# GpSimd subtracts the least of each late round, ScalarE takes four heads' exponentials at once, and the passage and the second norm are ordered anew

## The reference

```python
# 1. neighbourhood attention, 8 heads of 16, window 7 x 7, gate, residual, norm with gain and bias
attn = einsum(q, kn) + rpb_bias;  a = softmax(attn over the 49 keys)
y = x + (einsum(a, vn) @ proj_w + proj_b) * sigmoid(relu(x @ g1_w + g1_b) @ g2_w + g2_b)
t = norm(y) * ln_g + ln_b
# 2. additive attention over the 1024 tokens of an image, on n = norm(t)
h = tanh(q[:, :, None, :] + k[:, None, :, :] + bh)      # 32 units for each pair of tokens
e = einsum('biju,u->bij', h, Wa) + ba
t = t + softmax(e) @ n
# 3. top-1 mixture of 8 experts (128 -> 512 -> 128, relu) with a capacity, on norm(t)
t = t + ffn(norm(t))
```

## Time and profile before

| | us |
|---|---|
| median of 3 runs (714.23 to 714.83) | 714.52 |
| the profiled execution | 713.9 |
| its span | 712.1 |

### The profile page before, as it was taken

The page is one execution under the profiler, slowest core; times in us unless marked ns, Lnnn a source line. Parts: engine busy times, 40 slices in busy tenths (PEclk is TensorE's granted clock), DMA queues, the critical chain, the costliest instruction groups (busy, mean ns, idle before and its releaser), DMA issues.

```text
span 712.1 us, 12354 instructions
## 1 busy us (share of the span) xinstructions
PE 548.5 (77%) x4512; PEld 272.0 (38%) x4512; DVE 516.3 (73%) x1442; ACT 571.3 (80%) x364; POOL 506.1 (71%) x588
## 2 busy tenths in 40 slices
PE   6997835999898969798939577676776666758994
PEld 3665621434343434354304122221231222237783
DVE  2677767877989797888865896977878778633456
ACT  3675637899999997999977999999999999920531
POOL 1002167997979778998998998989798798611474
PEclk9999975999999989899988899999999999977998
DMA  8600100100000000000800000000000000001400
GB/s 307 211 2 2 60 1 1 60 1 5 1 12 3 12 0 14 1 9 5 323 0 13 0 12 9 5 12 1 13 9 4 12 10 5 10 3 34 132 25 27
DMA packets 14108, 24.32 MB, mean 34 GB/s; under 512 B 1296, under 2 KB 11058, under 8 KB 13024
## 3 DMA queue, kind: packets, MB, share of 16 engines
q1 hardware_dynamic: 12640, 20.63, 8.5%
q0 software_dynamic: 1408, 2.91, 1.2%
HBM read 16.79 MB, written 7.37 MB: 34 GB/s over the span
## 4 chain that ended last, share of the span: by engine, by line
PE 32%; issue 21%; DVE 21%; ACT 17%; POOL 8%; DMA 1%; DVEq 0%; POOLq 0%; SPq 0%; ACTq 0%
ACT front L1148 15%; PE ps L895 9%; POOL front L581 5%; DVE front L1427 5%; PE ps L693 3%; PE ps L1056 3%; PE ps L1046 3%; PE ps L915 2%; DVE back L1236 2%; PE ps L722 2%; PE ps L741 2%; PE ps L732 1%; DVE back L1263 1%; POOL y_all L540 1%; PE ps L938 1%
## 5 line engine op out<-in xcount | busy, mean ns | idle before, releaser
L1148 ACT ACTIVATE front<-front 128x4096 f32<-128x4096 f32 x128 | 454.9, 3605 | 36.8 <-POOL front L581 24.9
L581 POOL TENSOR_SCALAR front<-k,q 128x1024 f32<-128x1024 f32 (+1 forms) x464 | 413.5, 908 | 42.3 <-PE ps L895 33.5
L895 PE MATMUL ps<-front,cst 128*32 128x512 f32 x2048 | 261.0, 630 | 80.4 <-ACT front L1148 73.5
L1427 DVE TENSOR_SCALAR front<-ps,q 128x512 f32<-128x512 f32 (+1 forms) x256 | 213.8, 878 | 22.0 <-PE ps L895 17.4
L895 PEld LDWEIGHTS ps<-front,cst 128*32 128x32 f32 x2048 | 55.9, 113 | 200.3 <-ACT front L1148 99.8
L1088 ACT ACTIVATE back<-back,mn 128x320 f32<-128x320 f32 (+1 forms) x128 | 62.4, 537 | 14.2 <-DVE mn L1236 14.2
L540 POOL TENSOR_SCALAR y_all<-y_all,mvs,lny 128x128 f32<-128x128 f32 x15 | 11.7, 786 | 74.2 <-DVEq L1392 58.9
L1236 DVE CUSTOM_DVE_ANT_0 back<-ps,back 128x320 f32<-128x320 f32 (+1 forms) x128 | 54.0, 469 | 12.5 <-PE ps L693 10.4
L1459 DVE COPY ptm<-ps 128x512 f32<-128x512 f32 x32 | 22.1, 692 | 38.2 <-PE ps L906 36.7
L693 PE MATMUL ps<-conv 32*128 32x320 f32 (+1 forms) x256 | 38.3, 477 | 4.9 <-DVE mn L1236 4.8
L1263 DVE COPY back<-ps 128x512 f32<-128x512 f32 x44 | 30.2, 686 | 7.5 <-PE ps L732 7.3
(11 more groups left out here) (146 smaller groups left out, 658.9 us busy)
## 6 DMA issues: line engine op xcount, KB each, us to landing
back<-in_w SPq DMA_DIRECT2D x2, 2048.0 KB, 10.8
xbuf<-rec SPq DMA_DIRECT2D x1, 2720.0 KB, 21.3
back<-in_top SPq DMA_DIRECT2D x2, 1024.0 KB, 6.2
back<-in_bottom SPq DMA_DIRECT2D x2, 1024.0 KB, 6.5
front<-xbuf SPq DMA_DIRECT2D x2, 720.0 KB, 7.0
back<-in_inner SPq DMA_DIRECT2D x1, 1280.0 KB, 10.6
back<-in_b SPq DMA_DIRECT2D x1, 1280.0 KB, 16.1
xT<-in_xT SPq DMA_DIRECT2D x4, 256.0 KB, 6.4
```

The lines of the kernel that those rows point to most:

```text
L581: last = nc.gpsimd.tensor_scalar(ring[u % DEPTH][:, at + lo:at + hi], k4[:, img * L + k0 + lo:img * L + k0 + hi], q4[:, m:m + 1], 1.0, ALU ...
L895: last = nc.tensor.matmul(bank(to)[c * U:(c + 1) * U, :], c_("wa", U - QPG - QPG * row, 2 * U - QPG - QPG * row), ring[t % DEPTH][:, at:at ...
L1148: nc.scalar.activation(ring[t % DEPTH], ring[t % DEPTH], ACT.Tanh).then_inc(h_ready, 1)
L1427: last = nc.vector.tensor_scalar(ring[u % DEPTH][:, at + lo:at + keys], ps[:, base + k0 + lo:base + k0 + keys], q4[:, m:m + 1], None, ALU.add)
```

## The change

- Passage: units 0 and 4 (`BIASED`) have no sums; ScalarE takes their tanh from the keys with the query as bias, in eight operations of 512. The transposes of the first four rows and their copy move from round 15 to round 14. The first keys are copied by VectorE from another bank. VectorE's part ahead of the loop is a list of its own, and the steps before 0 are gone; the loops begin at step 0, and on GpSimd and VectorE at step 1.
- Second norm: rows 4 and 5 are GpSimd's, 6 and 7 VectorE's; 8 to 11 as before but a row per step on GpSimd; 12 and 13, then 14, on GpSimd; 15 on VectorE. Tokens and keys of the last pack are turned four steps earlier, and image 1's units may have sums from `project_step(15)` + 5 on instead of + 9.
- Late rounds: GpSimd computes (least - score) for each head (`below_most`), two heads in step begin+1 and two in begin+2, after the step's sums; ScalarE then has one exponential over the four heads, in step begin+3.

```diff
+BIASED = (0, CH // 2)
 def sums_at(t):
-    gate = lambda u: FIRST if u < NEW_KEYS[1] else KEYS_1 if u < NEW_KEYS[2] else project_step(NB - 1) + 9
-    return [u for u in range(T) if max(u - DEPTH + 1, gate(u)) == t]
+    gate = lambda u: KEYS_1 if u < NEW_KEYS[2] else project_step(NB - 1) + 5
+    return [u for u in range(NEW_KEYS[1] + 1, T) if max(u - DEPTH + 1, gate(u)) == t]
...
-        middle, late_rows = project_step(11), project_step(NB - 1)
+        rows_8, rows_12, rows_14, rows_15 = (project_step(j) + 1 for j in (11, 13, 14, 15))
...
# GpSimd
-            scale_rows(2, 4, 7)
-            weigh_rows("lng", ALU.mult, 4, 7)
-            weigh_rows("lnb", ALU.add, 4, 7, done=True)
+            scale_rows(2, 4, 6)
+            weigh_rows("lng", ALU.mult, 4, 6)
+            weigh_rows("lnb", ALU.add, 4, 6, done=True)
...
+            def below_most(rho, pair):
+                n = KEYS[kind_of(rho // 2)]
+                pool.wait_ge(n_ready, NG * rho + 2 * pair + 2)
+                for g in range(2 * pair, 2 * pair + 2):
+                    p = prob[rho % 3][:, g, 0:n]
+                    last = nc.gpsimd.tensor_scalar(p, p, mn[rho % 3][:, g:g + 1], -1.0, ALU.subtract, ALU.mult)
+                last.then_inc(below_ready, 1)
...
-            for t in range(FIRST, END):
+            key_query_sums(1)
+            key_query_sums(2)
+            normal_rows(2, 4, 6)
+            key_query_sums(3)
+            for t in range(KEYS_1, END):
...
+                for pair in range(2):
+                    rho = round_at(t - 1 - pair, begin)
+                    if rho is not None:
+                        below_most(rho, pair)
-                if t == middle + 4:
-                    scale_rows(3, 8, 12)
+                if rows_8 + 2 <= t < rows_8 + 6:
+                    scale_rows(3, t - rows_8 + 6, t - rows_8 + 7)
...
# TensorE, after the early rounds
+            pe.wait_ge(n_ready, NG * RS)
+            query_columns(0, 1)
             values(RS - 1)
-            query_columns(0, 1)
+            key_half(0, 2)
+            sums(BS - 1)
+            query_key_rows("wqe", 2, 3, q_done)
+            spread(BS - 1)
+            pe.wait_ge(pta_ready, chunks_before(RS) - RS)
+            query_key_rows("wqo", 2, 4, q_done)
+            project(BS - 1)
             pe.wait_ge(ptd_ready, RS)
-            pe.wait_ge(pta_ready, chunks_before(RS) - RS)
-            key_half(0, 5)
-            query_key_rows("wqe", 2, 2, q_done)
-            query_key_rows("wqo", 2, 3, q_done)
-            query_key_rows("wk", 2, 4, k_done)
+            query_key_rows("wk", 2, 5, k_done)
...
# ScalarE
+                if t in BIASED:
+                    ...
+                    for at, k0, keys, m, _, _ in tiles_of_unit(t):
+                        last = nc.scalar.activation(ring[t % DEPTH][:, at:at + keys], k4[:, k0:k0 + keys], ACT.Tanh,
+                                                    bias=q4[:, m:m + 1])
+                    last.then_inc(h_ready, 1)
+                    return
...
+            def soften_late(rho):
+                p = prob[rho % 3][:, :, 0:KEYS[kind_of(rho // 2)]]
+                act.wait_ge(below_ready, 2 * (rho - RS) + 2)
+                nc.scalar.activation(p, p, ACT.Exp).then_inc(p_ready, NG)
...
-                rho = round_at(t - 2, begin)
-                if rho is not None:
-                    soften(rho, (0, 1))
                 rho = round_at(t - 3, begin)
                 if rho is not None:
-                    soften(rho, (2, 3))
+                    soften_late(rho)
...
# VectorE, ahead of its loop
+            keys_out(0, 2)
+            inverse(BS - 1)
+            dve.wait_ge(ln_rows, 2)
+            dve.wait_ge(y_ready, 7)
+            row_stats(4, 7)
+            scaled(BS - 1)
+            key_query_sums(1)
+            gated(BS - 1)
+            dve.wait_ge(y_ready, BS)
+            row_stats(7, 8)
+            scale_late(0, 4, 8)
+            dve.sem_inc(ln_last, 1)
+            link.end()
+            normal_rows(y_all, 6, 8)
+            key_query_sums(2)
+            weigh_rows(6, 8)
+            row_stats(6, 8)
+            key_query_sums(3)
+            scale_late(0, 6, 8)
+            link.end()
+            normal_rows(x_all, 6, 8)
+            dve.sem_inc(t_ready[1], 1)
```

More of the change, by code:

```diff
@@ L189, in sums_at, with summed @@
 def sums_at(t):
-    gate = lambda u: FIRST if u < NEW_KEYS[1] else KEYS_1 if u < NEW_KEYS[2] else project_step(NB - 1) + 9
-    return [u for u in range(T) if max(u - DEPTH + 1, gate(u)) == t]
+    gate = lambda u: KEYS_1 if u < NEW_KEYS[2] else project_step(NB - 1) + 5
+    return [u for u in range(NEW_KEYS[1] + 1, T) if max(u - DEPTH + 1, gate(u)) == t]
+def summed(u):
+    return u + 1 - sum(k <= u for k in BIASED)
 def leasts_before(n):
@@ L447, in keys_whole, with keys_bank @@
             return GROUPS[GROUP_AT[u]].half is None
-        KEYS_NEEDED = [1, 2, 4]
+        KEYS_NEEDED = {BIASED[0] + 1: 1, BIASED[1] + 1: 2, T // 2: 4}
+        def keys_bank(u):
+            g = GROUPS[GROUP_AT[u]]
+            return 2 * 512 if g.block >= BPI or g.half == 0 else 4 * 512
         def pool_part(u, n):
@@ L610, in _ @@
                     normed(p)
[L611 to L613 removed]
+                for pair in range(2):
[4 more added lines that the diff above has]
+                    scale_rows(3, t - rows_8 + 6, t - rows_8 + 7)
+                if t == rows_8 + 6:
                     weigh_rows("lng", ALU.mult, 8, 12)
[L615 removed]
+                if t == rows_8 + 7:
                     weigh_rows("lnb", ALU.add, 8, 12, done=True)
[L617 to L625, removed]
+                if rows_8 + 10 <= t < rows_8 + 14:
+                    normal_rows(3, t - rows_8 - 2, t - rows_8 - 1)
+                if rows_12 + 1 <= t < rows_12 + 3:
+                    scale_rows(4, t - rows_12 + 11, t - rows_12 + 12)
+                if t == rows_12 + 3:
+                    weigh_rows("lng", ALU.mult, 12, 14)
+                    weigh_rows("lnb", ALU.add, 12, 14, done=True)
+                if rows_12 + 5 <= t < rows_12 + 7:
+                    normal_rows(4, t - rows_12 + 7, t - rows_12 + 8)
+                if t == rows_14 + 1:
+                    scale_rows(5, 14, 15)
+                    weigh_rows("lng", ALU.mult, 14, 15)
+                    weigh_rows("lnb", ALU.add, 14, 15, done=True)
+                if t == rows_14 + 3:
+                    normal_rows(5, 14, 15)
             def weighted_bias(q):
@@ L820, in turn_tokens @@
             def turn_tokens(half, to):
-                pe.wait_ge(t_ready[half], 2 if half == 1 else 1)
+                pe.wait_ge(t_ready[half], (1, 2, 4, 4)[half])
                 for k in range(4):
@@ L938, in keep_clock @@
                     nc.tensor.matmul(bank(3, 0, P), c_("ident"), c_("tri"), start=True, stop=True)
-            for t in range(FIRST, END):
+            for t in range(END):
                 rho = round_at(t, begin)
@@ L1156, in soften_main @@
                 nc.scalar.activation(pm[:, lo:L], pm[:, lo:L], ACT.Exp, bias=nmin[:, :], scale=-1.0).then_inc(pm_ready, 1)
-            for t in range(FIRST, END):
-                if 0 <= t < T:
+            for t in range(END):
+                if t < T:
                     hidden_units(t)
+                if t == 0:
+                    query_rows(1, 0, 0, 3)
+                    query_rows(1, 0, 1, 4)
+                    act.wait_ge(k_done, 3)
+                    nc.scalar.activation(kT[:, 0:512], bank(5), ACT.Identity, bias=c_("bk")).then_inc(k_ready, 1)
                 p = query_block(t, 2)
@@ L1533, in _ @@
                 if t == KEYS_1:
-                    tokens_out(1, 2)
+                    tokens_out(1, 3)
                     dve.wait_ge(q4_done, 2)
-                    nc.vector.tensor_scalar(q4[:, P:2 * P], bank(3, 0, P), c_("bh"), None, ALU.add).then_inc(q4_ready, 1)
+                    nc.vector.tensor_scalar(q4[:, P:2 * P], bank(2, 0, P), c_("bh"), None, ALU.add).then_inc(q4_ready, 1)
                     keys_out(1, 5)
```

166 lines of the change are left out of this document (74 added, 92 removed).

## The result

The changed kernel takes 780.12 us (median of 4 runs, 775.75 to 781.94) against 714.67 of the kernel before: 1.090 times (95% interval 1.086 to 1.095). The forecast was 718.6 us with 710.5 to 731 as its range. The direction was right and the size off by 61 us: what came is rival 2 in its dearer form, 785 us.

The account below looks back on a forecast made before the run. GpSimd's queue was taken to set unit 64's tanh start: 117.6 + 272.8 work + 8 idle = 398.4 us, 4.1 later than before. With the rest fixed, 718.6 us as a median, range 710.5 to 731.

Parts of the forecast that it names:

- rival 2: Late rounds: GpSimd's subtraction carries the extra 0.43 us, 746 us, or costs per element, 785 us; chance 0.13.
- What bounds: Whole kernel: unit 64's tanh start, 394.3 us before, sets the end; GpSimd is last to be ready from about 268.
- the sum of 272.8: GpSimd's work in us from unit 5's sums to the end of unit 64's sums, including 31.8 of subtractions.
- rival 3: PE loses its clock in longer gaps, GpSimd's ring waits, 15 us idle: 725.6 us; chance 0.12.
- the price of the subtraction: Late rounds on GpSimd: 0.51 us for 320 elements, 0.46 for 256, 31.8 us in all, priced like a product.
- its own upper bound of 4.2 ns per element: Late rounds: if subtraction costs per element, 0.25 + 320 x 4.2 ns = 1.6 us per operation, +66 us.
- The ends of ScalarE: Late rounds: one exponential over 1280 takes 1.25 us instead of four at 1.80, saving 9 us over 16 rounds.
- The wait that it adds: Late rounds: ScalarE's exponential waits for GpSimd's list; GpSimd sets the pace at 0.7 us more per three units, 12 rounds.
- The passage: Ahead of unit 5: rows ready at 109.3 instead of 116.88, GpSimd's sums start at 117.6, 5.1 us sooner.
- "nothing, with +-0.7": Round 14's added transposes and copy, with VectorE's chain moved earlier: no net time, bounds +-0.7 us.
- The norms: Rows 8 to 15: GpSimd 16.1 instead of 17.2 us; VectorE's four more chains hidden except PE's waits for small results.
- Idle time: GpSimd until unit 64: 8 us idle taken, with 2 and 15 as ends; break-even at 3.9.

Follow-up runs that it names:

- e3: Changed kernel with GpSimd adding the least and multiplying by 1.0 instead of subtract-multiply, exponential scale -1.0 (another output): 737.83 us, 1.032 times the kernel before.
- e5: Changed kernel with the same exponents by another form, GpSimd multiplying by -1.0 and then adding the least: 737.42 us, 1.031 times the kernel before.
- e2: Changed kernel with the late rounds put back: no GpSimd subtractions, four ScalarE exponentials with bias, new passage and norms kept: 722.43 us, 1.011.
- e8: Changed kernel with cheap add-multiply operations on unused GpSimd memory; one exponential per round waits only for VectorE's scores (another output): 728.13 us, 1.018.
- e6: Kernel before with the new passage alone, norms of rows 8 to 15 and late rounds as before: 708.14 us, 0.989.
- e9: Changed kernel where GpSimd subtracts nothing and only signals; one exponential per round waits for that signal (another output): 720.54 us, 1.006.
- e10: Changed kernel without the late rounds' change, with the last four rows' transposes and keys three steps later: 720.73 us, 1.008.
- e7: Changed kernel without the late rounds' change, rows 12 to 15 in one GpSimd pack as before, last keys four steps later: 709.56 us, 0.990.
- e4: Kernel before with the late rounds' change alone, passage and norms as before: 775.48 us, 1.084.
- e1: Kernel before with nine forms of GpSimd scalar operation added in its idle time, over 128 and 512 elements: subtract-multiply 3.35 ns per element, add- or multiply-first 0.84.

## Why the prediction was wrong

- **What bounds** was right, and the frame of the sum too: the end is unit 64's start and a fixed rest (232.8 us of tanh and softmax). GpSimd's busy time between 119.16 and 456.70 is 321.6 us; the sum of 272.8 with the subtraction repriced gives 323.4. PE's lower granted clock (rival 3) was there, 0.85 in this stretch, but all of GpSimd's idle time, by which alone it could act on the sum, is 15.9 us.
- **The step that failed** is the price of the subtraction: "I take 0.51, since form and pointers of the product match". It was 1.34 from start to start (1.37 recorded) for 320 elements and 1.13 for 256, so 82.4 us in place of 31.8: 50.6 of the 58 us by which unit 64 was missed (456.7 against 398.4). The prediction had the row that said so, the normalisation's 0.78 for 128 elements, and its own upper bound of 4.2 ns per element stood near the 3.35 measured. It chose by the form of the operands; the arithmetic operation decides. By this alone e3 and e5 are 42.3 and 42.7 us faster, of the 65 that were lost. With a chance of 0.13 for rival 2 the case was seen and underrated, and the range left it out.
- The Trainium skill's rule (GPSIMD Engine Reference, Performance versus the Vector engine: up to two ALU operations per element are bound by the port at 1.03 cycles per element) stood beside it. The product and the add-multiply agree, at 0.83 and 0.84 ns per element. Subtract-multiply has two operations too and takes four times that, and one operation alone takes three times that; for these the measurement decides against the rule.
- **The ends of ScalarE** were right: one exponential over 1280 released it after 1.18 us (159.66 to 160.84), against 1.25 said. It bought nothing, since ScalarE waited 85 us before these operations.
- **The wait that it adds** was described as it happened for ScalarE, but its rate counted only GpSimd's busy time, 0.7 us per three units. With cheap operations, as the prediction had them, e2, e8 and e3 show 5.7 us for the work and 9.7 more through the wait (9.5 and 6.6 by the stretches). In the changed kernel GpSimd had no wait for the ring between unit 5's sums and 400 us, so there the price of the operation is nearly all.
- **The passage** was right in kind: by e6 7.9 us of the time. In the changed kernel its start for GpSimd was 119.2 instead of 117.6. The first keys were copied at 94.45 on VectorE where ScalarE had them at 92.29 before, 2.2 us later; VectorE's list behind them took 16.3 us instead of 15.7, and the rows were ready at 111.6 instead of 109.3. Unit 1's energies, 2.60 us instead of 3.41, gave part of it back. Whether "nothing, with +-0.7" for round 14 was wrong stays open: with the same code up to there, e9's and e10's unit 0 began 2.5 and 3.0 us sooner than the changed kernel's, at a granted clock of 1.00 instead of 0.76 from 77 to 91 us.
- **The norms** were said to be hidden except for PE's small results. That exception, with row 15's transposes, is 12.9 us by e2 against e7. In the changed kernel it is GpSimd's one long wait of 9.6 us; it took back what the passage had gained, and the changed kernel came out 4.6 us above e4.
- **Idle time** of GpSimd: 15.9 us (337.5 - 321.6), just above the range of 2 to 15, 7.9 more than the 8 that were taken. The wait of 9.6 us is more than that excess. With 1.6 of a later start, and 1.8 less busy time than the repriced sum, this is the rest of the miss of unit 64: 50.6 + 7.9 + 1.6 - 1.8 = 58.3.

## What to carry to other kernels

Price an operation that moves to another engine by a row with the same arithmetic operation there, not by one with the same operands; where the nearest rows disagree by a factor, measure nine forms in an idle stretch before building on one. An engine that is behind also holds what waits at the end of its list, so a small product for another engine belongs ahead of the long work of the step: 7.2 us here. And count small dependent chains by who waits for them: four more roots and the products of row 15, put on an engine that was busy three quarters of the time, cost 13 us because PE stood before them with the energies behind.

## What the hardware showed that was not expected

GpSimd's scalar operations have three speeds in float32 in e1. Add-multiply, multiply-multiply and multiply-add with two scalars run at 0.83 to 0.84 ns per element, subtract-multiply at 3.35. A form with one scalar and no second operation is slow as well, subtract and add alike: 600 and 604 ns for 128 elements, 1558 and 1565 for 512, 2.5 ns per element. So an addition is made faster there by multiplying with 1.0 behind it (368 and 692 ns), which this kernel's sums had done all along. A second pointer costs 0.07 to 0.08 us.
